# Second-layer residuals taken in two pairs, and three rows of source scores spread by DMA instead of by TensorE

## The chip, the cores and the metric

The kernel runs on one core of a Trainium2 chip. Its time is the device time of one execution in microseconds (us), median of several. The engines are TensorE (PE, with its weight load PEld), VectorE (DVE), ScalarE (ACT), GpSimd (POOL) and the SyncE queue (SP), which here only issues DMAs.

## The reference: three layers of graph attention with layer norms

For each of B = 16 graphs of N = 512 nodes (x is [16, 512, 256], the adjacency is [16, 512, 512]):

- Layer 1, four heads of 128 features: xl = x @ W1, a source score asrc and a target score adst per node and head. For each target d the scores leaky_relu(asrc[s] + adst[d]) over the sources s are masked by the adjacency (the diagonal always allowed) and go through a softmax over s; the head's output is the weighted sum of the sources' xl. Bias, then elu.
- Layer 2, one head of 256 features over the 512 features of layer 1, same form, plus bias; its result is added to x and layer-normed to x1.
- Layer 3: Wh = x1 @ W, the same kind of masked softmax (no diagonal, over the other axis), leaky; added to x1 and layer-normed to the output.

## The kernel before, in words

The program is written out by hand as a software pipeline over slots, six per batch n. At slot 6n + pos the unit that is "current" is: pos 0 the third layer of batch n-3 ("L3"), pos 1 to 4 the heads h0 to h3 of batch n, pos 5 the second layer of batch n-1 ("L2"). A unit is one attention matrix of 512 by 512. There is no planner: each engine has its own loop over the slots, which issues its instructions in a fixed order, and semaphores tie the engines together. An engine never overtakes its own order.

What happens to a unit g:

1. TensorE, end of slot g-2: `sources_row` (L410; the shared helper `spread` at L403 to L408 issues the instructions, so they show as L407) makes a row of the unit's 512 source scores, the same in all 128 partitions, in PSUM bank bA: four transposes of a score column broadcast to 128 by 128. It waits until the unit before has read bA.
2. VectorE, slot g-1: `tops` (L751) takes four 128x512 tensor_tensor_reduce instructions (L757): masked maximum over the row, with inputs mask_t (SBUF, bf16) and bA (PSUM, f32). Then `shifted_targets` (L770, L775) turns the maxima into a column b_t with two instructions on 128x4 operands, all in SBUF.
3. TensorE, middle of slot g-1: `targets_row` (also L407, into bank bB) spreads b_t. It stands before other work of the slot in TensorE's order.
4. ScalarE, slot g: leaky (L608), exp (L619). VectorE, slot g: `keep_edges` (L801) masks.
5. TensorE, slot g+1: `attend` in two halves (L447 heads, L458 second layer, L468 third layer). Between the halves stand the turning of an older head (L437), the next `targets_row`, and pieces of the layers' products: values_1 (L540, L543), values_2 (L516), values_3 (L504), the turning of the masks (L529) and of x1 (L495).

The attention outputs go to four PSUM banks bU0 to bU3, used in rotation; each use waits until the reader of the use four before is done. In slot pos 0 TensorE attends the L2 unit: target blocks d = 0 and 1, the turning of head 2, then d = 2 and 3: five uses. So d = 3 waits until `second_out` has written the residual of d = 0, `res1` (L828). In the kernel before, VectorE does `second_out` for all four blocks in slot pos 1, ahead of `tops(h1)`.

VectorE's order at pos 0: tops(h0), make_mask (L805), x_low (L810), invert_3 (L815: the third layer's softmax sums), low_part of head 2 (L794), elu (L782). At pos 1: second_out, tops(h1), keep_edges(h0), norm_stats. At pos 2: low_part of head 3, tops(h2), keep_edges(h1), norm_1 (L845, writes x1n). At pos 3: invert of h0 (L788, which needs the last half of its attention), tops(h3), keep_edges(h2).

GpSimd's order: scale_3 (L362: multiplies the third layer's values by z3inv, four tensor_scalar; TensorE's attend of L3 at pos 1 waits for all four), norm_scale (L337, L340), then, gated by x1n: residual_2 (L376), set_diag (L368) and add_bias_2 (L354), three tensor_tensor instructions back to back, and later norm_2 (L346).

SyncE's order in iteration n: load_adj(n+2) after make_mask(n+1), load_x(n+2) after res1 of batch n-2, then the store of the output of batch n-3.

Of the kernel before, what the change touches and what calls it, by code (L numbers as in the profile page):

```python
# [5 lines left out]
P = 128  # L6
# [19 lines left out]
class Unit:  # L26


    def __init__(self, kind, batch, index, slot):
        self.kind = kind  # L30
        self.batch = batch
        self.index = index
        self.slot = slot
        self.row = kind != "L3"


def gat_kernel(nc, x, adj, W1, as1, ad1, b1, W2, as2, ad2, b2, W3, a3, out):
# [26 lines left out]
        u.r = i  # L64
    for u in units.values():
        u.h = H * u.batch + u.index

    def head_at(slot):
        u = units.get(slot)
# [2 lines left out]
    with ExitStack() as ctx:  # L72
        def sb(name, shape, dt=F32):
            return ctx.enter_context(nc.sbuf_tensor(name, shape, dt))
# [4 lines left out]
        def sem(name):  # L79
            return ctx.enter_context(nc.semaphore(name))  # L80
# [46 lines left out]
        act3 = sb("act3", [P, NB, D])  # L127
        y_out = act3
        res2 = sb("res2", [P, NB, D])
        junk = sb("junk", [P, NB, N], BF16)  # L130
        top = [sb(f"top{i}", [P, NB]) for i in range(2)]
        low = sb("low", [P, NB])
# [34 lines left out]
        bias2_ready = sem("bias2_ready")  # L167

        adj_loaded = sem("adj_loaded")
        x_loaded = [sem(f"x_loaded{i}") for i in range(4)]  # L170
        out_stored = sem("out_stored")

# [99 lines left out]
        @block.sync  # L272
        def _(sp):
            def load_adj(n):
                if n:
                    sp.wait_ge(mask_made, n)
                sp.dma_start(adj_in[:], adj[n].rearrange("(b p) s -> p b s", p=P)).then_inc(adj_loaded, 16)

            def load_x(n):
                if n >= 4:  # L280
                    sp.wait_ge(res1_done, (n - 3) * NB)
                sp.dma_start(x_in[n % 4][:], x[n].rearrange("(b p) f -> p b f", p=P)).then_inc(x_loaded[n % 4], 16)

            for k in range(KD):
                for g in range(G):
                    sp.dma_start(w1[:, k, g, 0:HC].rearrange("p (c n) -> p c n", n=FX)[:, :, 0:F],
                                 W1[k * P:(k + 1) * P, g * HW:(g + 1) * HW].rearrange("p (c n) -> p c n", n=F))\
                        .then_inc(w1_in, 16)
            sp.dma_start(att1s, as1.rearrange("(o h) f -> o (h f)", o=1).to_broadcast([P, HF])).then_inc(w1_in, 16)
            sp.dma_start(att1d, ad1.rearrange("(o h) f -> o (h f)", o=1).to_broadcast([P, HF])).then_inc(w1_in, 16)  # L290
            load_x(0)
            load_adj(0)
            b1_row = b1.rearrange("(o n) -> o n", o=1)
            sp.dma_start(b1_in[0:1, :], b1_row).then_inc(b1_loaded, 16)
            sp.dma_start(b1_in[32:33, :], b1_row).then_inc(b1_loaded, 16)
            sp.dma_start(w2[:, :, 2:DX], W2.rearrange("(k p) n -> p k n", p=P)).then_inc(w23_in, 16)
            sp.dma_start(att2s, as2.to_broadcast([P, DO])).then_inc(w23_in, 16)
            sp.dma_start(att2d, ad2.to_broadcast([P, DO])).then_inc(w23_in, 16)
            sp.dma_start(w3[:, :, 2:DX], W3.rearrange("(k p) n -> p k n", p=P)).then_inc(w23_in, 16)
            sp.dma_start(att3, a3.rearrange("(o a) c -> o (a c)", o=1).to_broadcast([P, 2 * DO])).then_inc(w23_in, 16)  # L300
            sp.dma_start(bias2[:], b2.rearrange("(o a) -> o a", o=1).to_broadcast([P, DO])).then_inc(w23_in, 16)
            load_x(1)
            for n in range(-1, B + 3):
                if 1 <= n + 2 < B:
                    load_adj(n + 2)
                if 2 <= n + 2 < B:
                    load_x(n + 2)
                if 0 <= n - 3 < B:
                    sp.wait_ge(y_out_done, (n - 2) * NB)
                    sp.dma_start(out[n - 3].rearrange("(b p) f -> p b f", p=P), y_out[:]).then_inc(out_stored, 16)  # L310
            sp.wait_ge(out_stored, 16 * B)
# [84 lines left out]
        def _(pe):  # L396
# [13 lines left out]
            def sources_row(u):  # L410
                if u.kind == "h":
                    pe.wait_ge(val1_ready, (u.batch + 1) * NB)
                elif u.kind == "L2":
                    pe.wait_ge(val2_ready, (u.batch + 1) * NB)
                else:
                    pe.wait_ge(val3_ready, (u.batch + 1) * NB)
                if u.u:
                    pe.wait_ge(top_done, u.u * NB)
                spread(bA, lambda b: a_col(u, b), arow_done)

            def targets_row(u):
# [133 lines left out]
            for g in range(FIRST, LAST + 1):  # L555
                n, pos = divmod(g, SLOTS)
                before, after, later = (units.get(g + i) for i in (-1, 1, 2))
                oldest = head_at(g - 3)
                third, second, batch = 0 <= n - 2 < B, 0 <= n - 1 < B, 0 <= n + 1 < B
                if g == 0:  # L560
                    weight_sums()
                if pos == 0 and batch:
                    turn_x(n + 1)
                if pos == 1 and batch:
                    turn_masks(n + 1)
                if pos == 2 and batch:
                    values_1(n + 1, 1)
                if pos == 3 and second:
                    values_2(n - 1, (2, 3))
                if pos == 4 and third:  # L570
                    values_3(n - 2, (0, 1))
                if pos == 5 and batch:
                    values_1(n + 1, 2)
                if before:
                    attend(before, 0)
                if oldest:
                    turn_head(oldest)
                if after and after.row:
                    targets_row(after)
                if pos == 1 and batch:  # L580
                    if n == -1:
                        pe.wait_ge(w1_lo_ready, 1)
                        pe.wait_ge(bias1_ready, 2 * G)
                    values_1(n + 1, 0)
                if pos == 2 and second:
                    if n == 1:
                        pe.wait_ge(w2_lo_ready, 1)
                    values_2(n - 1, (0, 1))
                if pos == 3 and third:
                    turn_x1(n - 2)  # L590
                if pos == 4 and third:
                    values_3(n - 2, (2, 3))
                if pos == 5 and batch:
                    values_1(n + 1, 3)
                if before:
                    attend(before, 1)
                if later:
                    sources_row(later)

        @block.scalar  # L600
# [141 lines left out]
        def _(dve):  # L742
# [7 lines left out]

            def tops(u):  # L751

                dve.wait_ge(arow_done, u.u + 1)
                if u.kind == "h" and u.index == 0:
                    dve.wait_ge(mt_ready, 2 * (u.batch + 1))
                for b in range(NB):
                    nc.vector.tensor_tensor_reduce(junk[:, b] if u.row else att[u.slot % 3][:, b], mask_t[u.batch % 4][:, b],  # L757
                                                   bA[:], 1.0, a_col(u, b) if u.row else LOWEST, ALU.add, ALU.max,
                                                   top[u.u % 2][:, b:b + 1]).then_inc(top_done, 1)

            def shifted_targets(u):
# [52 lines left out]
                dve.wait_ge(exp3_done, (m + 1) * NB)  # L814
                nc.vector.reciprocal(z3inv[:], z3[:]).then_inc(z3inv_ready, 1)  # L815

            def second_out(u):
                m = u.batch
                dve.wait_ge(xb_done, m + 1)
                if m:  # L820
                    dve.wait_ge(x1n_done, m * NB)
                for pair in range(0, NB, 2):
                    for d in (pair, pair + 1):
                        dve.wait_ge(att2_done, m * NB + d + 1)
                        nc.vector.reciprocal(z2inv[:, d:d + 1], bU[(u.use[d // 2] + d % 2) % 4][:, DO:DO + 1]).then_inc(z2inv_ready, 1)
                    for d in (pair, pair + 1):
                        dve.wait_ge(z2inv_ready, m * NB + d + 1)
                        nc.vector.scalar_tensor_tensor(res1[:, d], bU[(u.use[d // 2] + d % 2) % 4][:, 0:DO], z2inv[:, d:d + 1],  # L828
                                                       x_in[m % 4][:, d], ALU.mult, ALU.add).then_inc(res1_done, 1)

            def norm_stats(m, which, res, res_sem, per, stats_sem, moments_sem):
                for b in range(NB):
# [60 lines left out]
            for g in range(FIRST, LAST + 1):  # L893
# [5 lines left out]
                if older:  # L899
                    invert(older)  # L900
                if pos == 1 and units.get(g - 2):
                    second_out(units[g - 2])
                if last_head:
                    low_part(last_head)
                if after:
                    tops(after)
                    shifted_targets(after)
                if g == 0:
                    shift_bias_2()
                if pos == 0 and 0 <= n + 1 < B:  # L910
# [40 lines left out]
```

## Time and profile before

| | |
|---|---|
| median of 3 runs | 1030.2 us (1029.69 to 1033.57) |
| profiled execution | 1028.2 us, its span 1026.4 us |
| granted TensorE clock, mean | 0.969 |
| PE busy / DVE / ACT / POOL, share of span | 87% / 73% / 70% / 26% |

The span is the time from the first to the last instruction; the execution's own time is 1.8 us more. A busy share is an average over the whole span. The chain of waits is the list of pieces of work, each released by the one before it, that leads to the last instruction. In a row, "[a <-X]" means that the engine sat idle for a us before this instruction and that X released it.

### The profile page before, as it was taken

To read this page: it belongs to the slowest core of one execution; us is meant where nothing else is said; L and a number is where in the kernel's file an instruction comes from. 1 tells how busy PE (TensorE), PEld (TensorE's weight loads), DVE (VectorE), ACT (ScalarE), POOL (GpSimd) and SP (SyncE) were. 2 spreads that over 40 slices of the span, in tenths; PEclk is the share of its full clock that TensorE was granted. 3 is DMA by queue.
4 is the path that set the end of the run, shared out by engine and by line. 5 is a ranking of instruction groups with operands and counts; after the bars stand their busy time and mean duration, and the time that the engine had idled before them with its cause. 6 is when DMAs were issued, how large, how long until landed. Compare 5 with 4: busy or idle time off the path is not lost.

```text
span 1026.4 us, 17742 instructions
## 1 busy us (share of the span) xinstructions
PE 896.5 (87%) x6472; PEld 835.7 (81%) x6472; DVE 744.7 (73%) x1875; ACT 716.7 (70%) x1299; POOL 271.3 (26%) x257
## 2 busy tenths in 40 slices
PE   1787889998999999998999999898999999998663
PEld 1676879897989989898988989798998989796553
DVE  5657687787787878778787878777787878775430
ACT  1476868777686877778686877778686877875530
POOL 1001001123232313223232412323231412424433
PEclk9998999999999999999999999999999999999886
DMA  7201020202011020202001020201001000000000
GB/s 212 71 1 63 1 62 2 62 2 70 14 41 43 5 79 1 82 2 64 20 26 58 1 82 1 83 1 62 22 22 63 1 21 2 21 1 21 21 21 21
DMA packets 28185, 37.18 MB, mean 36 GB/s; under 512 B 962, under 2 KB 19522, under 8 KB 28100
## 3 DMA queue, kind: packets, MB, share of 16 engines
q1 hardware_dynamic: 28100, 36.05, 11.0%
q8 instruction: 53, 0.87, 0.4%
q14 instruction: 32, 0.26, 0.1%
HBM read 27.66 MB, written 8.39 MB: 35 GB/s over the span
## 4 chain that ended last, share of the span: by engine, by line
PE 40%; ACT 27%; DVE 22%; issue 8%; POOL 2%; DMA 1%; SPq 0%; POOLq 0%; DVEq 0%; ACTq 0%
PE bU L468 11%; ACT att L619 6%; PE bU L447 6%; PE bG L516 6%; DVE junk L757 6%; ACT att L608 5%; PE bG L543 5%; ACT x L631 4%; PE bU L458 4%; DVE att L801 4%; ACT att L623 3%; DVE low L770 2%; PE bB L407 2%; DVE y_lo L794 2%; DVE stats L834 2%
## 5 line engine op out<-in xcount | busy, mean ns | idle before, releaser
L447 PE MATMUL bU<-val,att 128*128 128x129 f32 x2048 | 249.7, 275 | 3.2 <-DVE att L801 3.2
L801 DVE TENSOR_TENSOR att<-att,mask_n 128x2048 f32<-128x2048 f32 x80 | 183.4, 2292 | 94.9 <-ACT att L619 94.7
L757 DVE CUSTOM_DVE_ANT_0 junk<-mask_t,bA,val 128x512 bf16<-128x512 bf16 x320 | 219.8, 743 | 39.8 <-PE bA L407 36.2
L447 PEld LDWEIGHTS bU<-val,att 128*128 128x128 f32 x2048 | 241.5, 192 | 5.6 <-issue 3.4
L608 ACT ACTIVATE att<-bB,val 128x512 f32<-128x512 f32 x320 | 202.3, 707 | 1.3 <-PE bB L407 1.3
L458 PE MATMUL bU<-val,att 128*128 128x257 f32 x512 | 129.1, 403 | 43.0 <-DVE res L828 33.5
L619 ACT ACTIVATE att<-att 128x2048 f32<-128x2048 f32 x80 | 155.2, 1940 | 0.2
L458 PEld LDWEIGHTS bU<-val,att 128*128 128x128 f32 x512 | 99.1, 201 | 63.3 <-DVE res L828 39.6
L468 PE MATMUL bU<-val3s,att 128*128 128x256 f32 x512 | 118.7, 386 | 10.3 <-POOL val3s L362 10.3
L468 PEld LDWEIGHTS bU<-val3s,att 128*128 128x128 f32 x512 | 97.1, 194 | 23.1 <-issue 10.5
L337 POOL TENSOR_SCALAR var_eps<-moments 128x4 f32<-128x4 f32 x32 | 6.2, 194 | 407.6 <-DVE moments L837 407.6
L631 ACT ACTIVATE x<-bU,zinv 128x128 f32<-128x128 f32 x256 | 73.2, 375 | 46.6 <-DVE zinv L788 46.5
L346 POOL TENSOR_SCALAR act<-res,moments,rstd 128x256 f32<-128x256 f32 x64 | 100.8, 1584 | 1.8
L671 ACT COPY val<-bG 128x524 f32<-128x524 f32 x64 | 38.6, 604 | 75.2 <-PE bG L543 75.1
L516 PE MATMUL bG<-w_hi,y_hi 128*128 128x258 f32 x256 | 75.3, 294 | 0.0
L543 PE MATMUL bG<-w_hi,x_hi 128*128 128x262 f32 x256 | 74.7, 292 | 0.0
L543 PE MATMUL bG<-w_lo,x_hi 128*128 128x262 f32 x256 | 74.6, 291 | 0.0
L543 PE MATMUL bG<-w_hi,x_lo 128*128 128x262 f32 x256 | 74.5, 291 | 0.0
L376 POOL TENSOR_TENSOR res<-act,x1n 128x1024 f32<-128x1024 f32 x16 | 37.9, 2372 | 133.6 <-DVE x1n L845 115.0
L516 PE MATMUL bG<-w_hi,y_lo 128*128 128x258 f32 x256 | 72.4, 283 | 0.0
L516 PE MATMUL bG<-w_lo,y_hi 128*128 128x258 f32 x256 | 72.3, 282 | 0.0
L407 PE MATMUL bB<-ident,b_t 128*128 128x128 f32 x320 | 49.7, 278 | 19.8 <-DVE b_t L775 19.8
(87 smaller groups left out, 1643.4 us busy)
## 6 DMA issues: line engine op xcount, KB each, us to landing
adj_in<-in_adj_dram SPq DMA_DIRECT2D x16, 1024.0 KB, 5.3
x_in<-in_x_dram SPq DMA_DIRECT2D x16, 512.0 KB, 3.9
out_dram<-act SPq DMA_DIRECT2D x16, 512.0 KB, 2.9
att<-in_L_gnn_W_dram SPq DMA_DIRECT2D x4, 128.0 KB, 2.5
att<-in_L_gnn_W_dram SPq DMA_DIRECT2D x1, 512.0 KB, 8.5
att<-in_L_gnn_att_src_dram SPq DMA_DIRECT2D x1, 256.0 KB, 4.6
att<-in_L_gnn_att_dst_dram SPq DMA_DIRECT2D x1, 256.0 KB, 6.0
w<-in_L_gnn_W_dram SPq DMA_DIRECT2D x1, 256.0 KB, 7.0
```

The costliest lines, as they stand in the source:

```text
L346: nc.gpsimd.tensor_scalar(y_out[:, b], res2[:, b], moments[:, 1, b, 0:1], rstd[:, 1, b:b + 1], ALU.subtract, ALU.mult).then_inc(y_out_done, 1)
L407: ins = nc.tensor.transpose(bank[:, b * P:(b + 1) * P], column(b).to_broadcast([P, P]), ident[:])
L447: ins = nc.tensor.matmul(to[:, (d % 2) * FX:(d % 2 + 1) * FX], p[:, s, d * P:(d + 1) * P], val1[u.batch % 2][:, s, u.index // 2, values], ...
L458: ins = nc.tensor.matmul(to[:, 0:DO + 1], p[:, s, d * P:(d + 1) * P], val2[:, s, 2:DX + 1], start=(s == 0), stop=(s == NB - 1))
L468: ins = nc.tensor.matmul(to[:, d * DO:(d + 1) * DO], p[:, j, (2 * i + d) * P:(2 * i + d + 1) * P], val3s[:, j], start=(j == 0), stop=(j == ...
L516: ins = nc.tensor.matmul(g_bank(b % 2)[:, 0:DX], left[:, k, nodes], right[:, k], start=(k == 0 and i == 0), stop=(k == KH - 1 and i == 2))
L543: ins = nc.tensor.matmul(to, left[:, k, nodes], right[:, k, g], start=False, stop=(k == KD - 1 and i == 2))
L608: nc.scalar.activation(p[:, b], bB[:], ACT.Prelu, bias=a_col(u, b), alpha=SLOPE)\
L619: nc.scalar.activation(flat(p), flat(p), ACT.Exp).then_inc(exp_done, 1)
L631: nc.scalar.activation(x1[u.h % 2][:, d * P:(d + 1) * P], bU[u.use[d // 2] % 4][:, (d % 2) * FX:(d % 2) * FX + F], ACT.Copy, scale=zinv[u. ...
L757: nc.vector.tensor_tensor_reduce(junk[:, b] if u.row else att[u.slot % 3][:, b], mask_t[u.batch % 4][:, b], bA[:], 1.0, a_col(u, b) if u.r ...
L801: nc.vector.tensor_tensor(flat(p), flat(p), mask_n[u.batch % 3][:, 0:NB * N], ALU.min).then_inc(prob_done, 1)
```

## The change

1. `second_out` takes a pair of target blocks. Blocks 0 and 1 of the L2 unit are now taken in VectorE's slot pos 0, after tops(h0) and its shifted_targets and before make_mask; blocks 2 and 3 stay at pos 1, where all four were.
2. For heads h1, h2, h3 TensorE no longer makes the sources' row. When the four value blocks of a batch are in SBUF (val1_ready), SyncE stores the three score columns to a DRAM scratch of 4 x 512 f32, waits for the stores, and loads them back spread over the 128 partitions into an SBUF tile a_rows. `tops` of those heads reads its row from there instead of from bA, after waiting for a_spread. h0, L2 and L3 keep TensorE's row; their wait on bA is counted among themselves.

```diff
+        self.by_dma = kind == "h" and index > 0
...
+        a_rows = sb("a_rows", [P, H, N])
+        a_dram = nc.dram_tensor("a_rows_dram", (H, N), F32).ap()
...
+            def spread_rows(n):
+                sp.wait_ge(val1_ready, (n + 1) * NB)
+                if n:
+                    sp.wait_ge(a_spread, 16 * n)
+                for h in range(1, H):
+                        sp.dma_start(a_dram[h].rearrange("(b p) -> p b", p=P),
+                                     val1[n % 2][:, :, h // 2, HC + h % 2]).then_inc(a_stored, 16)
+                sp.wait_ge(a_stored, (n + 1) * (H - 1) * 16)
+                if n:
+                    sp.wait_ge(top_done, (units[SLOTS * (n - 1) + H].u + 1) * NB)
+                sp.dma_start(a_rows[:, 1:H].rearrange("p h n -> p (h n)"),
+                             a_dram[1:H].rearrange("(o h) n -> o (h n)", o=1).to_broadcast([P, (H - 1) * N]))\
+                    .then_inc(a_spread, 16)
...
                 if 2 <= n + 2 < B:
                     load_x(n + 2)
+                if 0 <= n + 1 < B:
+                    spread_rows(n + 1)
                 if 0 <= n - 3 < B:
...
-                if u.u:
-                    pe.wait_ge(top_done, u.u * NB)
+                before = [v for v in units.values() if not v.by_dma and v.a == u.a - 1]
+                if before:
+                    pe.wait_ge(top_done, (before[0].u + 1) * NB)
...
-                if later:
+                if later and not later.by_dma:
                     sources_row(later)
...
-                dve.wait_ge(arow_done, u.u + 1)
+                if u.by_dma:
+                    dve.wait_ge(a_spread, 16 * (u.batch + 1))
+                else:
+                    dve.wait_ge(arow_done, u.a + 1)
+                a_row = a_rows[:, u.index] if u.by_dma else bA[:]
...
-                                                   bA[:], 1.0, a_col(u, b) if u.row else LOWEST, ALU.add, ALU.max,
+                                                   a_row, 1.0, a_col(u, b) if u.row else LOWEST, ALU.add, ALU.max,
...
-            def second_out(u):
+            def second_out(u, pair):
...
                 if pos == 1 and units.get(g - 2):
-                    second_out(units[g - 2])
+                    second_out(units[g - 2], 2)
...
                 if after:
                     tops(after)
                     shifted_targets(after)
+                if pos == 0 and units.get(g - 1):
+                    second_out(units[g - 1], 0)
```

## Rows read from the trace of the kernel before

**Rows 1.** One steady batch: busy time of each engine; then TensorE's idle by releaser.

```profile
504.44:562.08 57.64, 54.23 (x407) 51.12 (x406) 45.93 (x113) 44.45 (x82) 17.22 (x16) 1.00 0.11 38
PE bU L458 <- DVE res L828: 33.5, 15, 2.5
```

**Rows 2.** Timeline of PE in that batch: start us, us, engine, line, what.

```profile
510.53 0.65 PE L407 MATMUL bB<-ident,b_t 128*128 128x128 f32 x4 [0.27 <-DVE b_t L775]
527.23 0.36 PE L540 MATMUL bG<-bias,ones_r 128*128 128x262 f32 x1 [0.66 <-ACT val L671]
532.12 3.64 PE L458 MATMUL bU<-val,att 128*128 128x257 f32 x16
540.84 2.00 PE L458 MATMUL bU<-val,att 128*128 128x257 f32 x8 [2.48 <-DVE res L828]
542.68 0.60 PE L407 MATMUL bA<-ident,val 128*128 128x128 f32 x4
543.12 1.06 PE L529 MATMUL bG<-ident_b,mask_n 128*128 128x128 bf16 x16
544.01 3.67 PE L468 MATMUL bU<-val3s,att 128*128 128x256 f32 x16
```

**Rows 3.** Chain of waits, the stretch after head 3's maxima: start us, us, what.

```profile
508.40 1.88 DVE low L770
510.31 0.17 DVE b_t L775
...
540.33 0.47 DVE res L828
```

**Rows 4.** Timeline of DVE, same batch.

```profile
505.61 0.75 DVE L757 CUSTOM_DVE_ANT_0 junk<-mask_t,bA,val 128x512 bf16<-128x512 bf16 x1 [0.27 <-PE bA L407]
538.40 0.18 DVE L815 RECIPROCAL z3inv<-z 128x4 f32<-128x4 f32 x1 [0.51 <-ACT att L623]
543.74 0.74 DVE L757 CUSTOM_DVE_ANT_0 junk<-mask_t,bA,val 128x512 bf16<-128x512 bf16 x1
560.57 1.37 DVE L845 TENSOR_SCALAR x1n<-res,moments,rstd 128x256 f32<-128x256 f32 x4
562.80 0.17 DVE L788 RECIPROCAL zinv<-bU 128x2 f32<-128x2 f32 x1 [0.78 <-PE bU L447]
```

**Rows 5.** Timeline of POOL, same batch.

```profile
504.44 2.37 POOL L376 TENSOR_TENSOR res<-act,x1n 128x1024 f32<-128x1024 f32 x1 [8.98 <-DVE x1n L845]
506.77 1.16 POOL L368 TENSOR_TENSOR mask_n<-mask_n,ident_big 128x512 bf16<-128x512 bf16 x1
507.89 2.36 POOL L354 TENSOR_TENSOR x_in<-x_in,bias 128x1024 f32<-128x1024 f32 x1
538.68 2.31 POOL L362 TENSOR_SCALAR val3s<-val,z3inv 128x256 f32<-128x256 f32 x4 [6.36 <-DVE z3inv L815]
```

**Rows 6.** Start of the program: two DVE reductions on SBUF inputs, and POOL's instruction there.

```profile
24.52 0.42 DVE L746 CUSTOM_DVE_ANT_0 junk<-att 128x256 bf16<-128x256 f32 x1
24.99 1.36 DVE L746 CUSTOM_DVE_ANT_0 junk<-att 128x256 bf16<-128x256 f32 x1
24.91 1.15 POOL L368 TENSOR_TENSOR mask_n<-mask_n,ident_big 128x512 bf16<-128x512 bf16 x1 [21.95 <-PE bG L529]
```

**Rows 7.** ScalarE's last value copy, batch 0 and steady; head 1's first maximum in batch 0; DMAs.

```profile
36.49 0.59 ACT L671 COPY val<-bG 128x524 f32<-128x524 f32 x1 [2.13 <-PE bG L543]
43.87 0.73 DVE L757 CUSTOM_DVE_ANT_0 junk<-mask_t,bA,val 128x512 bf16<-128x512 bf16 x1
529.22 0.59 ACT L671 COPY val<-bG 128x524 f32<-128x524 f32 x1 [0.32 <-PE bG L543]
536.79 0.37 SPq L277 DMA_DIRECT2D adj_in<-in_adj_dram  x1
adj_in<-in_adj_dram SPq DMA_DIRECT2D x16, 1024.0 KB, 5.3
x_in<-in_x_dram SPq DMA_DIRECT2D x16, 512.0 KB, 3.9
```

More of the change, by code:

```diff
@@ L66, in gat_kernel @@
         u.h = H * u.batch + u.index
+    for i, u in enumerate(u for u in units.values() if not u.by_dma):
+        u.a = i
     def head_at(slot):
@@ L169, in gat_kernel @@
         adj_loaded = sem("adj_loaded")
+        a_stored = sem("a_stored")
+        a_spread = sem("a_spread")
         x_loaded = [sem(f"x_loaded{i}") for i in range(4)]
@@ L282, in load_x @@
                 sp.dma_start(x_in[n % 4][:], x[n].rearrange("(b p) f -> p b f", p=P)).then_inc(x_loaded[n % 4], 16)
+            def spread_rows(n):
[3 more added lines that the diff above has]
+                for h in range(1, H):
+                    with nc.allow_non_contiguous_dma(reason="columns of scores"):
+                        sp.dma_start(a_dram[h].rearrange("(b p) -> p b", p=P),
[6 more added lines that the diff above has]
+                    .then_inc(a_spread, 16)
             for k in range(KD):
@@ L815, in invert_3 @@
                 nc.vector.reciprocal(z3inv[:], z3[:]).then_inc(z3inv_ready, 1)
-            def second_out(u):
+            def second_out(u, pair):
                 m = u.batch
[L819 to L829, printed above, removed]
+                if pair == 0:
+                    dve.wait_ge(xb_done, m + 1)
+                    if m:
+                        dve.wait_ge(x1n_done, m * NB)
+                for d in (pair, pair + 1):
+                    dve.wait_ge(att2_done, m * NB + d + 1)
+                    nc.vector.reciprocal(z2inv[:, d:d + 1], bU[(u.use[d // 2] + d % 2) % 4][:, DO:DO + 1]).then_inc(z2inv_ready, 1)
+                for d in (pair, pair + 1):
+                    dve.wait_ge(z2inv_ready, m * NB + d + 1)
+                    nc.vector.scalar_tensor_tensor(res1[:, d], bU[(u.use[d // 2] + d % 2) % 4][:, 0:DO], z2inv[:, d:d + 1],
+                                                   x_in[m % 4][:, d], ALU.mult, ALU.add).then_inc(res1_done, 1)
             def norm_stats(m, which, res, res_sem, per, stats_sem, moments_sem):
```

## The prediction

> **What bounds the kernel now.** I read the page's shares first, then the stretch table of one steady batch, TensorE's timeline in it, the chain of waits, and last VectorE's and GpSimd's timelines side by side. A batch lasts 57.64 us and TensorE is busy 54.23 of them [rows 1]. Its idle time is three waits: 0.27 us for b_t of head 3, 0.66 us for a value copy, and 2.48 us at the last block of the second layer, which waits for the residual of block 0 to leave its bank [rows 2]. That third wait comes 15 times, 33.5 us in all [rows 1]. So TensorE is nearly the bound, but the chain of waits is on TensorE for only part of the batch. From head 3's `low` and b_t it runs over ScalarE and VectorE for 30.4 us (510.48, the end of b_t, to 540.84) until the residual releases the last block [rows 3]; from there it is TensorE's own work until the next head 3. The reader should keep this shape: two segments, A (from b_t of head 3 to the L2 unit) where VectorE and ScalarE hand work to each other without slack, and B (from there to head 3 again) where TensorE leads.
>
> **What the change takes off TensorE.** (a) The wait of 2.48 us: block 1 of the L2 unit is done at about 535.8 (532.12 + 3.64, [rows 2]), tops(h0) and its b_t end at 535.6 in the timeline, so the first pair's residuals are ready at about 536.8, before TensorE wants the bank at 538.4. (b) Three groups of four transposes a batch. TensorE's starts give the price: bA at 542.68, the next work at 543.12 [rows 2], 0.44 us each, 1.32 us in all. Together 3.8 us a batch, if nothing else becomes late.
>
> **What it adds on VectorE.** The first pair costs two reciprocals and two residuals, about 1.0 us (0.22 + 2 x 0.39, the spacing of the starts in the old place), and 0.2 us of waiting for block 1. VectorE had 0.51 us of idle before z3inv [rows 4]; the rest, about 0.75 us, pushes z3inv from 538.40 to 539.15, and with it GpSimd's four val3s, which took 2.31 us from 538.68 [rows 5]: now they end at 541.75 to 541.95. TensorE would want them at 541.15 (last block from 538.38 to 540.25, no bA row, 0.89 us of mask turning, the spacing of 543.12 and 544.01 in [rows 2]). So 0.6 to 0.8 us of the 2.48 comes back as a wait in front of L468; I take 0.8. At pos 1 the VectorE list gets shorter: tops(h1) starts at 541.6 instead of 543.74 [rows 4].
>
> **Segment B under the change.** From the start of the third layer's attention (544.01) to the end of x1n (560.57 + 1.37 = 561.94) took 17.9 us; one bA row less makes 17.5. From 542.0 that gives x1n at 559.4, 2.5 us earlier than before, and the last half of h0's attention, on which VectorE's invert waits (562.80, [rows 4]), comes at 560.3 instead of 562.8.
>
> **Where the gain meets something.** Behind x1n GpSimd runs three tensor_tensor instructions back to back, 5.8 us in all (504.44 to 510.25), and starts them 0.1 us after x1n [rows 5]. In the kernel before, tops(h3) ran right through them, its four instructions 0.67 us apart from 505.61 [rows 4], with one input from PSUM. But `low`, on four columns with both inputs in SBUF, took 1.88 us there [rows 3] against 0.17 us elsewhere, and ended with GpSimd's L354. And [rows 6] show the very instruction kind of `tops` with both inputs in SBUF: 0.42 us alone, 1.36 us when a GpSimd tensor_tensor of 1.15 us had started 0.08 us earlier. So a two-SBUF-input instruction of VectorE waits for a running GpSimd tensor_tensor, down to about 0.13 us before its recorded end. The change moves the row of tops(h3) from PSUM to SBUF, so now all four of its instructions are of that kind.
>
> The Trainium skill states this as a rule (SBUF — State Buffer, section "Who interferes with whom"): a VectorE instruction with two SBUF inputs contends with a GpSimd instruction that reads SBUF, and whichever issues first holds the shared pair for its whole instruction. The trace agrees, by [rows 6]; the page doesn't say who gets the pair when both have a queue of such instructions.
>
> The sum for head 3, counted from x1n at 559.4: GpSimd's first instruction starts at 559.45, VectorE asks at 560.35. If GpSimd keeps its queue going, its third ends at 565.2, and tops (2.7 us) plus low and b_t (0.4 us) end at 568.15. If the two engines take turns, the order is L376, t0, L368, t1, L354, t2, t3: 561.65 + 0.67 + 1.05 + 0.67 + 2.2 + 1.34 = 567.6, b_t at 568.0. Before, b_t(h3) ended at 568.12 (510.47 plus a batch). In both orders the 2.5 us that x1n gains is spent by the 2.7 us of tops that now stand behind GpSimd instead of beside it. b_t(h3) is the start of segment A, whose 30 us have no slack, so the batch stays at 57.5 to 57.7 us, and TensorE's wait reappears in front of head 3's targets row as 3.3 us. Before it was 0.27.
>
> The bounds of this one unknown: at the good end VectorE, once it has the port after L376, keeps it for all four (561.65 + 2.7 + 0.4: b_t at 564.75), TensorE leads again and the batch is 57.65 - 3.8 + 0.8 - 0.27, about 54.4 us. At the other end `tops` of h1 (from 541.6) also gets in front of the last of the four val3s (541.5 to 541.95), which costs TensorE up to 0.67 us more for each turn: 58.3 us. I take 57.6, since VectorE has an instruction of another kind between two tops (its read of the accumulator), where a waiting GpSimd instruction can step in, as L368 did in the gap between two reductions [rows 6].
>
> **The DMAs.** val1 is complete at 529.8 [rows 7]; tops(h1) wants its row at 541.6, and b_t(h1) has a further 1.1 us before TensorE reaches its targets row (545.9 against about 544.8). So the chain may take 11.8 us without a stall, 12.9 with one that nobody waits for. It is three issues at 0.37 [rows 7], 1.1 us; the stores' landing; an issue, 0.4; the spread's landing. The two loads, 512 packets of 1 KB in 3.9 and of 2 KB in 5.3 us [rows 7], give by their difference 1.4 us per 512 KB and some 2.5 us fixed: 4.6 us for the spread of 768 KB. The stores are 1536 packets of four bytes, 96 on each of 16 engines. No row shows such packets. At the least they cost the fixed 2.5 us, at the most, if each costs what a packet of 1 KB does (44 ns), 6.7 us. The chain is 8.6 to 12.8 us. I take 10.5: hidden. The queue behind it: the output store (was at 532.34) goes out at about 537 and lands well before ScalarE's third_out at 552.4, and the adjacency load is wanted a batch later. Batch 0 has no such cover: val1 at 37.1, tops(h1) at 43.9 [rows 7], so up to 3.5 us are lost once.
>
> The Trainium skill gives a minimum of 512 bytes for line rate, with read-modify-write below it (DMA: Bandwidth & Descriptors, section "Specifications"); that speaks for the upper end, and no run here shows it yet.
>
> **The sum.** The POOL triple stands behind x1n in 12 batches (213 to 850 us). There I count 0. The two batches before that and the ones after 850 have shorter L458 waits (1.4, 1.8 and 1.0 us in the timeline) and no or a short triple: about -5 us. The start costs +3.5. The sum is -1.5 us on the profiled 1028.2; carried to the median, 1030.2 - 1.5, about 1029.
>
> **The rivals.**
> - R1, VectorE keeps the port (or GpSimd's instructions don't hold it between each other): 12 x 3.25 = 39 us more, 990 us. For it: nothing in the trace shows who wins among queues, and GpSimd's val3s (tensor_scalar) slow down by 0.48 us beside an elu that isn't slowed. Against it: [rows 6].
> - R2, the slower side: the four-byte stores cost more than 45 ns each. From 12.9 us of chain on, each further us stands in front of tops(h1), whose b_t then comes after TensorE reaches targets(h1), and segment B starts no earlier, so all of it goes to the batch. At 60 ns a packet it is 1.5 us a batch, 15 batches: about 1050 us; at 90 ns, 1095. Against it: only that the rows' upper bound lies just below the threshold.
> - R3, the first pair isn't done earlier, because VectorE reaches it late: then the 2.48 us wait stays and the rows alone go, with head 3's tops behind GpSimd; about 1032. VectorE's 535.6 against TensorE's 538.4 speaks against it.
>
> **How the numbers follow.** 0.5% is about what a measurement of this kernel can tell from no change: 1025.0 to 1035.4. The forecast has 0.55 (its own range 1021 to 1038, from 57.4 to 58.3 us a batch: 0.14 of it faster, 0.31 same, 0.10 slower), R1 0.27, R2 0.15, R3 0.03 (same). So faster 0.41, same 0.34, slower 0.25. The range must take in R1's 990 with some room, and leaves out most of R2: 983 to 1038.
>
> **What would show it.** Right: the wait at L458 gone; a wait of about 3 us at targets(h3) (PE bB <- DVE b_t) in its place; L757 with a_rows with a mean far above 0.74 us in head 3 only, and equal to about 0.7 in h1 and h2; 0.6 to 0.8 us of PE waiting for val3s; SyncE's spread landing before 541.6 in batch terms. Wrong: a batch near 54.4 us with GpSimd's L368 and L354 stretched instead (R1); DVE waiting for the DMA of a_rows in front of every tops(h1) (R2); L458 still waiting for res (R3).

## The result, and the profile after

The changed kernel takes 1136.2 us (median of 4 runs, 1133.43 to 1142.44) against 1031.7 us before (4 runs): ratio 1.102, 95% interval 1.097 to 1.108. The forecast was 1029 us, with a range of 983 to 1038. The kernel became 10% slower instead. The profiled execution took 1134.2 us, its span 1132.4; the mean granted TensorE clock fell from 0.969 to 0.926.

The steady batch, from the start of GpSimd's residual_2 (L402 after, L376 before) to the next, averaged over 11 batches: 64.6 us ((949.19 - 238.69) / 11) against 58.1 us ((852.09 - 213.08) / 11, eight of them 57.6 and three 59.1 to 59.5). Eleven times 6.5 us are 71.5 of the 106 us that the profiled execution lost; 26 more are lost before the first of these batches and 9 after the last.

TensorE's larger waits over one batch's length, from head 1's targets row to the next head 1's, and the L2 unit, which no longer waits as it did in [rows 2] (start us, us, what, idle before and its releaser):

```profile
544.88 0.65 PE L433 MATMUL bB<-ident,b_t 128*128 128x128 f32 x4 [4.20 <-DVE b_t L806]
568.80 0.65 PE L433 MATMUL bB<-ident,b_t 128*128 128x128 f32 x4 [3.29 <-DVE b_t L806]
586.85 0.36 PE L567 MATMUL bG<-bias,ones_r 128*128 128x262 f32 x1 [0.34 <-ACT val L698]
596.09 3.64 PE L485 MATMUL bU<-val,att 128*128 128x257 f32 x16
601.28 3.69 PE L495 MATMUL bU<-val3s,att 128*128 128x256 f32 x16 [0.66 <-POOL val3s L388]
608.99 0.65 PE L433 MATMUL bB<-ident,b_t 128*128 128x128 f32 x4 [3.58 <-DVE b_t L806]
```

The last blocks of the L2 unit (596.09, sixteen matmuls in a row) run through where they waited 2.48 us. In its place stand two long waits for b_t: 544.88 and 608.99 are head 1's, 568.80 is head 3's. Behind head 1's stands the DMA. Timeline of the SyncE queue, of ScalarE's last value copy and of VectorE's first maximum of head 1, same batch:

```profile
588.85 0.59 ACT L698 COPY val<-bG 128x524 f32<-128x524 f32 x1 [0.32 <-PE bG L570]
589.47 1.47 SPq L299 DMA_DIRECT2D a_rows_dram<-val  x3
601.35 0.33 SPq L304 DMA_DIRECT2D a_rows<-a_rows_dram  x1
605.76 0.75 DVE L788 CUSTOM_DVE_ANT_0 junk<-mask_t,a_rows,val 128x512 bf16<-128x512 bf16 x1 [4.89 <-DMA a_rows<-a_rows_dram]
```

From the first store to the issue of the spread, which waits for the stores' landing, are 11.9 us (16 batches: 10.2 to 12.8, mean 11.6); the spread lands 4.4 us later. VectorE is ready at 600.9 and waits 4.89 us. The whole chain takes 16.3 us, where 12.9 was the point from which it costs. Over the run, from the view of waits (total, times, longest):

```profile
DVE junk L788 <- DMA a_rows<-a_rows_dram: 96.1, 16, 9.7
SPq L304 <- DMA a_rows_dram<-val: 160.6, 16, 11.3
```

Head 3, GpSimd's and VectorE's timelines:

```profile
560.14 2.40 POOL L402 TENSOR_TENSOR res<-act,x1n 128x1024 f32<-128x1024 f32 x1 [10.11 <-DVE x1n L876]
562.48 1.64 POOL L394 TENSOR_TENSOR mask_n<-mask_n,ident_big 128x512 bf16<-128x512 bf16 x1
564.07 2.79 POOL L380 TENSOR_TENSOR x_in<-x_in,bias 128x1024 f32<-128x1024 f32 x1
```

```profile
558.63 1.38 DVE L876 TENSOR_SCALAR x1n<-res,moments,rstd 128x256 f32<-128x256 f32 x4
560.96 2.13 DVE L788 CUSTOM_DVE_ANT_0 junk<-mask_t,a_rows,val 128x512 bf16<-128x512 bf16 x1
563.02 1.64 DVE L788 CUSTOM_DVE_ANT_0 junk<-mask_t,a_rows,val 128x512 bf16<-128x512 bf16 x1
564.59 2.83 DVE L788 CUSTOM_DVE_ANT_0 junk<-mask_t,a_rows,val 128x512 bf16<-128x512 bf16 x1
567.35 0.74 DVE L788 CUSTOM_DVE_ANT_0 junk<-mask_t,a_rows,val 128x512 bf16<-128x512 bf16 x1
568.59 0.16 DVE L806 SCALAR_TENSOR_TENSOR b_t<-top,low 128x4 f32<-128x4 f32 x1 [0.28 <-DVE low L801]
```

The records of the two engines overlap, and those that overlap are longer than the same instructions elsewhere (0.74 and 1.16 us), so a record holds the instruction's waiting for the port too. The four maxima took 2.7 us in [rows 4]; now 7.1. The first waits for L402, then L394 (1.64 instead of 1.16) waits for the first, the second for L394, and so on: the two engines take turns, one instruction each.

And a third thing: TensorE after such a wait. First stretches of the table by window (from:to, length, busy time and count of PE, PEld, DVE, ACT and POOL, then the granted clock as a share of 2.4 GHz, then the DMA's share and GB/s), then TensorE's own rows:

```profile
570.40:573.80 3.40, 3.40 (x21) 3.40 (x20) 1.36 (x3) 2.65 (x5) 0.00 (x0) 0.62 0.00 0
573.80:580.00 6.20, 6.20 (x44) 5.78 (x43) 4.72 (x13) 5.49 (x11) 0.00 (x0) 1.00 0.01 3
609.00:625.00 16.00, 16.00 (x123) 15.59 (x124) 12.54 (x28) 10.05 (x19) 3.53 (x3) 1.00 0.12 43
```

```profile
569.29 1.62 PE L522 MATMUL bG<-ident,x1n 128*128 128x128 f32 x8
570.71 3.05 PE L474 MATMUL bU<-val,att 128*128 128x129 f32 x16
575.78 1.95 PE L474 MATMUL bU<-val,att 128*128 128x129 f32 x16
```

The first two of these in the kernel before:

```profile
511.01 1.04 PE L495 MATMUL bG<-ident,x1n 128*128 128x128 f32 x8
511.89 1.95 PE L447 MATMUL bU<-val,att 128*128 128x129 f32 x16
```

The same sixteen matmuls take 1.95 us in a batch of the kernel before, here 3.05, and the eight turnings 1.62 instead of 1.04. After the idle stretch the clock is granted at its lower level, 1.2 GHz, for 3.4 us (the share of 0.62 is of a stretch that holds most of it) and then at 2.4 GHz again. That costs some 1.7 us more. It happens after head 1's wait at 544.88 too (0.62 in 546.50 to 549.90), but not after the one at 608.99, 3.58 us long: there the share is 1.00. In the eleven batches the share in the 4 us behind such a wait is at most 0.66 after 20 of 22 waits (head 1's of 3.6 to 5.7 us, head 3's of 3.0 to 3.3) and 1.00 after the other two. The two batches that hold only one fall are the shortest, 62.6 and 63.0 us; the nine others take 64.2 to 67.5.

What the clock takes can be read from two runs with the same 4315 matmuls in eleven batches, the changed kernel and a run below that has one spread and add_bias_2 moved, which has the clock share 1.00:

```profile
238.69:949.19 710.50, 617.85 (x4315) 582.85 (x4314) 532.44 (x1243) 489.77 (x892) 199.73 (x165) 0.94 0.15 44
225.62:843.45 617.83, 583.42 (x4315) 549.04 (x4314) 530.70 (x1243) 488.25 (x892) 199.90 (x166) 1.00 0.11 36
```

TensorE is busy 34.4 us longer: 3.1 us a batch, or 1.7 us for each of the 20 falls.

The batch adds up, by means over the eleven: 57.65, less 2.48 and 0.27 of old waits and 1.32 of rows, plus 0.66 (val3s), 4.3 (head 1), 3.1 (head 3) and 3.1 (clock): 64.7 us, measured 64.6.

### The profile page after: what moved, and what is told of

The parts are those of the page before. It is cut to its first block, busy times and chain, and to the rows that moved or that the text cites. A ratio compares the mean times of both kernels' runs of the same rounds, so it can differ in the third digit from the quotient of the medians.

```text
span 1132.4 us, 17404 instructions
## 1 busy us (share of the span) xinstructions
PE 913.5 (81%) x6280; PEld 853.0 (75%) x6280; DVE 778.2 (69%) x1875; ACT 718.0 (63%) x1299; POOL 283.2 (25%) x257
## 4 chain that ended last, share of the span: by engine, by line
PE 34%; DMA 23%; DVE 21%; ACT 13%; issue 5%; POOL 2%; SPq 1%; POOLq 0%; DVEq 0%; ACTq 0%
DMA a_rows_dram<-val 15%; DVE junk L788 13%; DMA a_rows<-a_rows_dram 8%; PE bG L570 7%; PE bU L474 7%; PE bU L495 6%; PE bG L543 5%; ACT att L635 3%; ACT att L646 3%; ACT x L658 3%; PE bB L433 3%; ACT val L698 2%; PE bU L485 2%; DVE stats L865 2%; PE bG L567 2%
## 5 line engine op out<-in xcount | busy, mean ns | idle before, releaser
L474 PE MATMUL bU<-val,att 128*128 128x129 f32 x2048 | 261.5, 283 | 3.7 <-DVE att L832 3.7
L474 PEld LDWEIGHTS bU<-val,att 128*128 128x128 f32 x2048 | 254.4, 200 | 6.1 <-issue 3.4
L788 DVE CUSTOM_DVE_ANT_0 junk<-mask_t,a_rows,val 128x512 bf16<-128x512 bf16 x192 | 189.8, 1043 | 96.1 <-DMA a_rows<-a_rows_dram 96.1
L433 PE MATMUL bB<-ident,b_t 128*128 128x128 f32 x320 | 55.7, 302 | 134.0 <-DVE b_t L806 134.0
L433 PEld LDWEIGHTS bB<-ident,b_t 128*128 128x128 f32 x320 | 38.7, 148 | 142.5 <-DVE b_t L806 142.5
L495 PE MATMUL bU<-val3s,att 128*128 128x256 f32 x512 | 124.2, 399 | 18.6 <-POOL val3s L388 17.9
L485 PE MATMUL bU<-val,att 128*128 128x257 f32 x512 | 122.3, 394 | 9.4 <-DVE att L832 9.4
L485 PEld LDWEIGHTS bU<-val,att 128*128 128x128 f32 x512 | 98.8, 198 | 23.9 <-DVE att L832 9.9
L788 DVE CUSTOM_DVE_ANT_0 junk<-mask_t,bA,val 128x512 bf16<-128x512 bf16 x128 | 87.8, 742 | 13.7 <-PE bA L433 11.1
L570 PE MATMUL bG<-w_hi,x_hi 128*128 128x262 f32 x256 | 80.2, 313 | 0.0
L570 PE MATMUL bG<-w_lo,x_hi 128*128 128x262 f32 x256 | 80.2, 313 | 0.0
L402 POOL TENSOR_TENSOR res<-act,x1n 128x1024 f32<-128x1024 f32 x16 | 38.2, 2386 | 147.5 <-DVE x1n L876 130.0
```

Of the source, the lines that this page charges most:

```text
L433: ins = nc.tensor.transpose(bank[:, b * P:(b + 1) * P], column(b).to_broadcast([P, P]), ident[:])
L474: ins = nc.tensor.matmul(to[:, (d % 2) * FX:(d % 2 + 1) * FX], p[:, s, d * P:(d + 1) * P], val1[u.batch % 2][:, s, u.index // 2, values], ...
L485: ins = nc.tensor.matmul(to[:, 0:DO + 1], p[:, s, d * P:(d + 1) * P], val2[:, s, 2:DX + 1], start=(s == 0), stop=(s == NB - 1))
L495: ins = nc.tensor.matmul(to[:, d * DO:(d + 1) * DO], p[:, j, (2 * i + d) * P:(2 * i + d + 1) * P], val3s[:, j], start=(j == 0), stop=(j == ...
L570: ins = nc.tensor.matmul(to, left[:, k, nodes], right[:, k, g], start=False, stop=(k == KD - 1 and i == 2))
```

## The experiments

All times are medians on the chip, each with its ratio to the kernel before run beside it. "Batch" is the steady batch as computed above. The changed kernel's is 64.6 us.

**Residual pairs alone.** The kernel before with second_out as in the change and nothing else:

```diff
-                    second_out(units[g - 2])
+                    second_out(units[g - 2], 2)
...
                     shifted_targets(after)
+                if pos == 0 and units.get(g - 1):
+                    second_out(units[g - 1], 0)
```

> Only the first half of the change: the residuals in two pairs; all source rows stay with TensorE. Theory (each term of the prediction holds by itself): the 2.48 us wait at L458 goes, about 0.35 us comes back at val3s (one bA group of 0.44 us stands between), head 3's tops still read PSUM, so x1n, GpSimd's triple and low all move with it: a batch of about 55.5 us, 1000 us in all, and no new wait in front of head 3's targets row beyond 0.3 us. Rival (segment A or GpSimd sets the batch whatever TensorE does): the wait moves to head 3 and the time stays at 1028 to 1032.

Measured: 992.4 us, ratio 0.965 (0.963 to 0.967), batch 55.3 us. TensorE's waits in a batch:

```profile
549.80 0.65 PE L407 MATMUL bB<-ident,b_t 128*128 128x128 f32 x4 [0.27 <-DVE b_t L775]
566.51 0.36 PE L540 MATMUL bG<-bias,ones_r 128*128 128x262 f32 x1 [0.66 <-ACT val L671]
580.94 3.69 PE L468 MATMUL bU<-val3s,att 128*128 128x256 f32 x16 [0.23 <-POOL val3s L362]
```

2.48 us gone, 0.23 come back, nothing moved elsewhere: 57.65 - 2.25 = 55.4. The total is 8 us better than expected, 5 of them since the kernel before also has three batches of 59.1 to 59.5 us and this one has none (all but one are 55.3). Those three are the clock: it falls behind their wait of 2.5 us and not in the eight others. In the table by window of the kernel before, one of them and the next:

```profile
213.08:272.41 59.33, 55.91 (x407) 52.23 (x406) 45.92 (x113) 44.45 (x82) 17.25 (x16) 0.97 0.12 36
272.41:330.06 57.65, 54.24 (x407) 51.13 (x406) 45.91 (x113) 44.46 (x82) 17.24 (x16) 1.00 0.12 38
```

So the wait of 2.48 us had a second cost in three batches of eleven, and it went with the wait. About 3 us of the difference stay unplaced. Half of the change is a clear gain.

**Rows by DMA alone.** The changed kernel with second_out whole at pos 1.

> Only the second half of the change: the rows of heads 1 to 3 by DMA; the residuals stay together at pos 1. Theory (the DMA chain of 16 us and the port at head 3 cost what they cost, whatever the pairs do): tops(h1) stood 13.9 us after val1, so the row is about 2 us late instead of 4 to 5, the L458 wait of 2.5 us stays, 3 us at head 3: a batch of 61 to 65 us, 1090 to 1140 us, no faster than the changed kernel by more than 2%. Rival (the pairs only fill time lost anyway, so the later tops(h1) hides the DMA): the time of the run with one spread, 1045.

Measured: 1130.0 us, ratio 1.0995 (1.096 to 1.103), batch 64.4. The L458 wait (here L485) is back, and yet the batch is the changed kernel's:

```profile
PE bU L485 <- DVE res L859: 28.7, 13, 2.5
DVE junk L788 <- DMA a_rows<-a_rows_dram: 59.9, 16, 9.4
```

So with the rows by DMA the pairs gain nothing: what they free, VectorE spends waiting for the row (59.9 us here, 96.1 there). The arrival of the DMA sets head 1 in both.

**One spread for batch 0, no DMA later.**

```diff
-                if 0 <= n + 1 < B:
-                    spread_rows(n + 1)
+                if n == -1:
+                    spread_rows(0)
...
-                    dve.wait_ge(a_spread, 16 * (u.batch + 1))
+                    dve.wait_ge(a_spread, 16)
```

> The changed kernel with the stores and the spread done for batch 0 alone; later batches read the same rows (their maxima are of other scores). So heads 1 to 3 read SBUF and no DMA is waited for. Theory (three terms in the changed kernel: late DMA, port turns at head 3, TensorE's clock after its waits): the DMA term goes, the port term stays: tops(h3) takes turns with GpSimd, 3.3 us of wait at its targets row, a batch of 57.6 us, or up to 1.7 us more if the clock falls after that one wait: 1027 to 1050 us. Rival (the DMA chain is all that is wrong): TensorE leads, 54.4 us a batch, 990 us. Second rival (the rows in SBUF cost in every head): L788 of heads 1 and 2 above 0.75 us and the time above 1060.

Measured: 1045.5 us, ratio 1.018 (1.015 to 1.020), batch 58.6. One long wait is left, at head 3:

```profile
525.33 1.12 PE L433 MATMUL bB<-ident,b_t 128*128 128x128 f32 x4 [3.25 <-DVE b_t L806]
```

and the stretch behind it in the table by window:

```profile
525.33:529.50 4.17, 4.17 (x24) 4.17 (x25) 2.25 (x2) 1.90 (x4) 0.00 (x0) 0.63 0.01 2
```

The wait has the forecast's size (3.3 us), and the clock falls behind it (0.63). Against the changed kernel the batch is 6.0 us shorter: that is what the late DMA costs, with the clock that falls behind its wait. Behind one of the eleven waits at head 3 (3.0 us at 642.11) the clock doesn't fall.

**The same, with head 3's row by TensorE.** `by_dma` for index 1 and 2 only.

> As the run before (one spread for batch 0, no DMA waited for later), but head 3's row is made by TensorE again and read from PSUM; heads 1 and 2 read SBUF. Theory: head 3's tops run beside GpSimd's triple again, the wait at its targets row is below 0.5 us, a batch of 55.0 us (57.65 - 2.48 - 0.88 + 0.7), 995 to 1000 us. Rival (head 3's delay has nothing to do with where the row lies): the wait of 3.3 us stays and the time is that of the run before.

Measured: 1001.6 us, ratio 0.974 (0.973 to 0.976), batch 54.9 against the expected 55.0, the wait at head 3 again 0.27. So where the row lies is what costs in head 3. The total is 2 us above the expected. Head 1 of batch 0 waits 9.9 us for the one spread, which may be the reason.

**The same as the run with one spread, with add_bias_2 moved.** GpSimd's L354 before the wait for x1n instead of behind set_diag.

> The run with one spread for batch 0, and GpSimd's add_bias_2 moved before the wait for x1n, so that two tensor_tensor instructions (2.4 and 1.2 us) instead of three stand beside tops(h3). Theory (tops(h3) takes turns with them): its four instructions take 2.2 us less in all, the wait at its targets row falls from 3.3 to about 1 us, the time from 1045 to 1005 to 1015. Rival (reading SBUF rows is slow in head 3 for another reason): no change from 1045.

Measured: 1014.7 us, ratio 0.986 (0.985 to 0.988), batch 56.2. Head 3's maxima in VectorE's timeline:

```profile
563.54 2.10 DVE L788 CUSTOM_DVE_ANT_0 junk<-mask_t,a_rows,val 128x512 bf16<-128x512 bf16 x1
565.57 1.64 DVE L788 CUSTOM_DVE_ANT_0 junk<-mask_t,a_rows,val 128x512 bf16<-128x512 bf16 x1
567.14 0.74 DVE L788 CUSTOM_DVE_ANT_0 junk<-mask_t,a_rows,val 128x512 bf16<-128x512 bf16 x1
567.81 0.74 DVE L788 CUSTOM_DVE_ANT_0 junk<-mask_t,a_rows,val 128x512 bf16<-128x512 bf16 x1
```

Two GpSimd instructions stretch two maxima, three stretched three. The wait at head 3 fell to 0.92 us. The instruction moved away now meets head 1 (0.83 us of wait there).

**One column of scores stored instead of three.** After batch 0, `for h in range(1, 2)` in the stores.

> The changed kernel, but after batch 0 only head 1's column is stored (512 four-byte packets instead of 1536); the spread still moves all 768 KB, with old rows for heads 2 and 3. Theory (each four-byte packet costs about 82 ns of its engine: (10.4 - 2.5) / 96): the stores land 5.7 us after val1 instead of 11.9, the spread at 10.2, before tops(h1) wants it: no wait for a_rows from batch 1 on, the time of the run with one spread. Rival (a store from SBUF to DRAM has a long fixed landing, the count is nothing): the store still takes 9 to 11 us, tops(h1) still waits 3 to 5 us, the time above 1100.

Measured: 1096.9 us, ratio 1.068 (1.064 to 1.072), batch 62.0.

```profile
579.88 0.37 SPq L299 DMA_DIRECT2D a_rows_dram<-val  x1
588.72 0.34 SPq L304 DMA_DIRECT2D a_rows<-a_rows_dram  x1
```

With a third of the packets the landing still takes 8.8 us here (16 batches, the first with three columns: 8.8 to 12.1, mean 9.6). The explanation by 82 ns for each packet has fallen. The recorded packets themselves are short: in the changed kernel's batch shown above all 1584 (with the semaphores' own) start within 1.46 us and take 7.9 ns each. What lasts is the time from there to the completion.

**Same bytes, same place, 512-byte packets.** The stores read four partitions of a tile of ones.

```diff
-                        sp.dma_start(a_dram[h].rearrange("(b p) -> p b", p=P),
-                                     val1[n % 2][:, :, h // 2, HC + h % 2]).then_inc(a_stored, 16)
+                    sp.dma_start(a_dram[h].rearrange("(b p) -> b p", p=P), ones[0:NB, :]).then_inc(a_stored, 16)
```

> The changed kernel with the three stores of the same 2 KB each to the same DRAM rows, but read from four partitions of a tile of ones: 4 packets of 512 bytes a store instead of 512 of four bytes (heads 1 to 3 then take maxima of a row of ones). So far: three stores need 11.6 us from first issue to the last landing, one store 9.3, though their packets have all gone by 1.5 us. Theory (DRAM takes long to acknowledge writes of four bytes): they land in 3 us after the last issue, 4.5 in all; the spread is there before tops(h1); time near 1045, that of the run with one spread. Rival (any store from SBUF followed by a wait needs 9 us): a_rows still late by 5 us, about 1136.

Measured: 1036.5 us, ratio 1.007 (1.004 to 1.009), batch 58.8.

```profile
593.77 0.95 SPq L298 DMA_DIRECT2D a_rows_dram<-ones  x3
595.63 0.35 SPq L302 DMA_DIRECT2D a_rows<-a_rows_dram  x1
```

1.9 us from first issue to landing instead of 11.9 (16 batches: mean 2.0); VectorE never waits for the row. The stores also read another tile, in four partitions instead of 128; the next run settles that this is not what counts.

**Four-byte packets, each 512 bytes from the next.**

```diff
-                        sp.dma_start(a_dram[h].rearrange("(b p) -> p b", p=P),
+                        sp.dma_start(a_pad[h][:, 0].rearrange("(b p) -> p b", p=P),
...
-                             a_dram[1:H].rearrange("(o h) n -> o (h n)", o=1).to_broadcast([P, (H - 1) * N]))\
+                             x[0, 0:(H - 1) * N // D].rearrange("(o a) f -> o (a f)", o=1).to_broadcast([P, (H - 1) * N]))\
```

> The changed kernel with the same four-byte packets, but each written to a DRAM place of its own, 512 bytes from the next, so that no two share a stretch of 512 bytes; the spread then loads 768 KB from x instead (other rows for heads 1 to 3). Theory A (neighbouring four-byte writes queue for one another in the same stretch of memory): landing in 3 to 4 us after the last issue, no wait for a_rows, time near 1045. Theory B (each write under some size is slow by itself, wherever it goes): landing as in the changed kernel, 10 us after the last issue, about 1136.

Measured: 1039.6 us, ratio 1.009 (1.005 to 1.014), batch 58.9.

```profile
596.57 1.47 SPq L299 DMA_DIRECT2D a_pad_dram<-val  x3
600.76 0.34 SPq L304 DMA_DIRECT2D a_rows<-in_x_dram  x1
```

4.2 us here, 3.2 to 4.2 over 16 batches (mean 3.6), with as many packets of four bytes from the same tiles. So neither their size nor their number nor reading them from SBUF takes the 10 us, but that they are neighbours in DRAM. Theory A holds in that, B falls. How near is too near isn't shown: the run puts each packet into a stretch of 512 bytes of its own and spreads them over 768 KB at once.

**A quarter of the columns at a time.** Each value block's three columns stored as soon as the block is ready.

```diff
+            def store_block(n, b):
+                sp.wait_ge(val1_ready, n * NB + b + 1)
...
+                        sp.dma_start(a_dram[h, b * P:(b + 1) * P].rearrange("(p o) -> p o", o=1),
+                                     a_col(Unit("h", n, h, 0), b)).then_inc(a_stored, 16)
```

> The changed kernel with each value block's three score columns stored when that block is ready (four times three stores of 128 packets), so that only the last block's 384 packets are left at the end. Theory A (neighbouring four-byte writes queue for one another): a quarter of the queue is left, landing about 4.5 us after the last issue, a_rows in time, 1045 to 1060. Theory B (a fixed answer time of some 9 us for such a write): nothing gained, 1130 to 1145.

Measured: 1093.1 us (ratio 1.062) and 1110.5 us in two runs, too few and too far apart for an interval, but both well under the changed kernel's lowest, 1133.4. Batch 61.4 in the first. The last two blocks' stores and the spread:

```profile
502.45 3.99 SPq L298 DMA_DIRECT2D a_rows_dram<-val  x6
513.73 0.32 SPq L308 DMA_DIRECT2D a_rows<-a_rows_dram  x1
```

From the end of the last issue (506.44) to the landing are 7.3 us here (16 batches: 7.2 to 9.8, mean 8.1), against 10.4 in the changed kernel (590.94 to 601.35; mean 10.1) and 8.5 to 11.1 with one column. Both theories missed: a quarter of the packets left at the end isn't a quarter of the time, and not all of it either. One reading is a queue for each stretch of 512 bytes: a block's column puts 128 four-byte writes into one stretch, and so does a whole column into each of its four. It explains why the number of columns counts for little, not why three take somewhat longer than one. That there is such a queue, and that its unit is 512 bytes, was argued, not tried.

**A hop through one SBUF partition.** The columns into one partition, then 6 KB in one store, then the spread; tops reads the row with a stride of four.

> The changed kernel with one hop more: the three columns go in four-byte packets into one SBUF partition (4 bytes each, target first, block second), from there in one store of 6 KB to DRAM, and then are spread; tops reads the row with a stride. All heads get their own rows. Theory (it is DRAM's answer to small writes that takes 9 us, and SBUF answers fast): 1.5 + 2.5 + 0.4 + 2.5 + 0.3 + 4.4 = 11.6 us from val1 to the spread, no or under 1 us of wait at tops(h1): 1045 to 1060. Rival (four-byte packets are slow to complete anywhere, or reading them from 128 partitions is): first hop 10 us, the chain 18 us, over 1160.

Measured: 1124.0 us in two runs (1118.7, 1129.2), ratio 1.092 (1.080 to 1.105), batch 63.7.

```profile
580.80 1.91 SPq L301 DMA_DIRECT2D a_line<-val  x3
587.74 0.25 SPq L304 DMA_DIRECT2D a_rows_dram<-a_line  x1
589.04 0.35 SPq L309 DMA_DIRECT2D a_rows<-a_rows_dram  x1
594.33 1.21 DVE L793 CUSTOM_DVE_ANT_1 junk<-mask_t,a_rows,val 128x512 bf16<-128x512 bf16 x1 [2.12 <-DMA a_rows<-a_rows_dram]
```

Two hops take 8.2 us instead of one of 11.9, the first 6.9 (expected 4.0), the second 1.3. So four-byte packets that land side by side in SBUF are slow too: 5.0 us behind the last issue, between the 10.4 of neighbours in DRAM and the 2.7 of packets set apart there. The wait for the row fell to 39.3 us in all, but the strided row makes each maximum 1.1 us long instead of 0.67, in all three heads. The run mixes two changes, so its time tells little; its landing times count.

**What rows by DMA could give.** Pairs, add_bias_2 moved, stores in 512-byte packets, heads 1 and 2 only.

> What rows by DMA could give at best: pairs, bias moved as above, rows of heads 1 and 2 alone by DMA, from stores of four 512-byte packets (of ones, so other rows), head 3's row by TensorE. Theory: TensorE has 0.88 us a batch less to do than in the pairs run but waits 0.4 us longer for val3s: a batch near 54.6, 980 to 995 us, within 1% of the pairs run: rows by DMA are worth next to nothing even when they are in time. Rival (TensorE is the bound and every transposition counts): 0.88 us a batch, 975 us or less.

Measured: 1002.0 us, ratio 0.974 (0.973 to 0.976), batch 55.4: 7 us above the expected, 1% slower than the pairs alone and 1.4% slower than the run that follows, which differs by the rows only. The 0.88 us of rows that TensorE saves are more than paid: it waits 0.84 us at head 1, where VectorE's second maximum is 2.83 us long beside the moved add_bias_2, and 0.66 us for val3s instead of 0.23.

**Pairs, with add_bias_2 moved.** No row by DMA.

> The kernel before with the residual pairs, no DMA rows, and GpSimd's add_bias_2 (L354, 2.36 us) moved from behind residual_2 and set_diag to before the wait for x1n. Theory: head 3's low no longer stands behind L354; but in the pairs run TensorE waited only 0.27 us there, so it gains that and no more: a batch of 55.0 us, 985 to 992 us. Rival (low's 1.9 us on the chain is a cost of its own): 1.5 us a batch, 970 us.

Measured: 988.6 us, ratio 0.9615 (0.9601 to 0.9630), batch 54.8: the best version here. The wait for b_t of head 3 is gone; the batch is 0.5 us shorter than with the pairs alone.

## Why the prediction was wrong

**The step that failed is a term of the sum: the landing of the four-byte stores.** The mechanism was named as rival R2, with 0.15: from 12.9 us of chain on, the delay stands in front of tops(h1). The bound of 6.7 us, from which the chain came out at 12.8 at most and 10.5 as taken, was made from packets of 1 KB, on the assumption that a packet of four bytes cannot cost more than one of 1 KB, and that the landing's fixed part is that of a load. The measured landing is 10.4 us behind the last issue (mean 10.1). Even R2 had a wrong reason: it counted time per packet on the DMA engines, but all packets have started within 1.5 us of the first, a third of them lands nearly as late, and the same packets with room between them land 2.7 us behind the last issue (mean 2.1). What makes the stores late is that the small writes are neighbours in DRAM; that they queue for one another there is the likely reason, and no run shows the queue itself.

The Trainium skill gives 512 bytes as the least for a transfer at full rate, with read-modify-write below it (DMA: Bandwidth & Descriptors, section "Specifications"). That pointed the right way, but here size by itself isn't it: the padded run has packets of four bytes and lands 2.7 us behind the last issue, three stores of 512-byte packets 0.9 us.

The error in the outcome is larger than this one term. R2 at 16.3 us of chain, by its own rule, gives 3.4 us a batch, so a batch of 61.0 and 1080 us. The measured batch is 3.6 us longer. Of these 3.1 are TensorE's clock, which the prediction didn't count at all: behind nearly every one of the two waits of over 3 us a batch it stands at 1.2 GHz for a time, 1.7 us each. Another 0.9 is head 1's wait, 4.3 us in the mean, and 0.4 go the other way (val3s and head 3). At the start the prediction counted 3.5 us for batch 0, and head 1 waits 9.7 there.

**What was right, step by step.**
- The 2.48 us at L458 go: right, and the pairs alone show their price to 0.1 us a batch.
- z3inv is pushed, val3s are late by 0.6 to 0.8: right, 0.66.
- Head 3: the maxima take turns with GpSimd's three instructions, b_t ends 8.6 us after x1n, TensorE waits 3.3: right, 8.7 (568.75 less 560.01) and 3.29. That kind of row ([rows 6]) was enough to forecast it. R1 (VectorE keeps the port) is excluded.
- The spread's landing, 4.6 by difference of two loads: right, 4.4.
- R3 is excluded: TensorE never waits for res in the changed kernel.
- "No change, if the DMA is in time": the 512-byte run is that case and is 0.7% slower (0.4% to 0.9%), batch 58.8 instead of 57.6. The clock after head 3's wait, in 10 of the 11 batches, takes 1.6 us a batch that the sum didn't have; the waits are 0.4 us shorter than the sum's (3.1 for 3.3 and 0.66 for 0.8).

**Where the chances went astray.** Of the prices that came only by bounds, this one had a threshold (12.9) within 0.1 us of its upper bound (12.8). A bound that close, and made of rows of another kind (large, aligned, reading), deserved far more than 0.15. The range ended at 1038 for that reason.

## What to carry to other kernels

Scattering a column of scores into a contiguous DRAM row cost 7 to 11 us of landing here, with one column as with three; plan on it, or write it in pieces of 512 bytes. A wait that replaces a TensorE stall of the same length isn't neutral: here nearly every stall of 3 us and more also took 1.7 us of clock. Moving an operand of VectorE from PSUM to SBUF can put the instruction into turns with GpSimd, so first look what GpSimd does at that time. And measure the two halves of a change apart: here one alone gives 3.5% and the other alone costs 10%.

## What the runs showed of the hardware that was not expected

- Behind the last issue, 512 four-byte writes into 2 KB of DRAM complete after 8.5 to 11.1 us, 1536 into 6 KB after 10.4 us (mean 10.1), the same 1536 placed 512 bytes apart after 2.7 us (600.76 less 598.04; mean 2.1), three stores of 512-byte packets after 0.9 us, and 1536 four-byte writes side by side in one SBUF partition after 5.0 us.
- VectorE and GpSimd, each with a row of instructions that read SBUF (two inputs on VectorE, tensor_tensor on GpSimd), alternate one by one in the batch shown, and the wait of 3.0 to 3.3 us behind it is in all eleven.
- After waits of 3.0 to 5.7 us TensorE's clock fell to 1.2 GHz in 20 of 22 cases in the changed kernel, in 10 of 11 with one spread and with 512-byte packets, and in 11 of 11 with padded ones; after waits of 2.5 us, in the kernel before, in 3 of 11. After waits of 1.2 us and less, in both DMA-row runs with add_bias_2 moved, it stayed at 2.4 GHz through all eleven batches (share 1.00). So the length of the wait alone doesn't decide it.
- An SBUF row of f32 read by tensor_tensor_reduce with a stride of four elements: 1.11 us instead of 0.67.
